# The last layer's attention over batches: one straight program, scores once per head, token-major softmax

## What is computed

```python
def _mha(x, Wqkv, bqkv, Wo, bo):        # L3_ffn: S = 4 batches, B = 512 tokens, H = 4, hd = 32
    qkv = x @ Wqkv.T + bqkv
    ...
    scores = jnp.einsum('bhqd,bhkd->bhqk', q, k) * (1.0 / np.sqrt(hd))
    att = jax.nn.softmax(scores, axis=-1)
    o = jnp.einsum('bhqk,bhkd->bhqd', att, v)
    return o @ Wo.T + bo
...
y = _layer_norm(x + _mha(x, Wqkv, bqkv, Wo, bo), g1, be1)
z = _layer_norm(y + _moe(y, Wg, W1, b1, W2, b2), g2, be2)
```

## Time and profile before

| | |
|---|---|
| median of 3 runs | 2115.09 us (2105.11 to 2148.61) |
| the profiled execution | 2104.8 us, span 2102.9 us |
| PE busy | 1673.5 us (80%), mean granted clock 0.858 |
| DVE busy | 1021.4 us (49%) |
| ACT busy | 722.8 us (34%) |
| POOL busy | 113.1 us (5%) |
| chain that ended last | PE 68%, DVE 20%, ACT 6%, issue 3% |

### The profile page before, as it was taken

The page is one execution under the profiler, slowest core; times in us unless marked ns, Lnnn a source line. Parts: engine busy times, 40 slices in busy tenths (PEclk is TensorE's granted clock), DMA queues, the critical chain, the costliest instruction groups (busy, mean ns, idle before and its releaser), DMA issues.

```text
span 2102.9 us, 22710 instructions
## 1 busy us (share of the span) xinstructions
PE 1673.5 (80%) x9040; PEld 701.1 (33%) x9046; DVE 1021.4 (49%) x2051; ACT 722.8 (34%) x1271; POOL 113.1 (5%) x167
## 2 busy tenths in 40 slices
PE   5559999888998879876489998888987798643385
PEld 2124333333433434322243233334334333211273
DVE  4564662424664641445656624336646414579312
ACT  2332553343343044333325533333430343311132
POOL 0000111000011000000001110000110000000302
PEclk9767999999898779978779998998997799856588
DMA  4000000000001000000000000000000000200141
GB/s 168 1 0 0 1 1 1 1 1 0 1 1 41 0 0 0 1 2 0 0 0 1 1 1 0 1 0 1 2 22 20 0 0 1 69 0 0 60 120 54
DMA packets 17387, 30.29 MB, mean 14 GB/s; under 512 B 1600, under 2 KB 12544, under 8 KB 16384
## 3 DMA queue, kind: packets, MB, share of 16 engines
q1 hardware_dynamic: 16256, 26.72, 3.8%
q0 software_dynamic: 1024, 2.10, 0.3%
HBM read 23.70 MB, written 5.11 MB: 14 GB/s over the span
## 4 chain that ended last, share of the span: by engine, by line
PE 68%; DVE 20%; ACT 6%; issue 3%; POOL 1%; DMA 1%; SPq 0%; POOLq 0%; DVEq 0%; ACTq 0%
PE ps L650 11%; PE ps L703 5%; PE ps L672 4%; PE ps L722 4%; PE ps L509 4%; PE ps L566 3%; PE ps L818 3%; PE ps L831 3%; PE ps L788 3%; PE ps L780 2%; PE ps L587 2%; PE ps L674 2%; PE ps L575 2%; PE ps L541 2%; ACT rs L1190 2%
## 5 line engine op out<-in xcount | busy, mean ns | idle before, releaser
L1255 ACT ACTIVATE big<-ps 128x512 f32<-128x512 f32 (+3 forms) x512 | 238.9, 515 | 257.3 <-PE ps L674 211.2
L650 PE MATMUL ps<-pp,qT 32*128 32x512 f32 (+3 forms) x1024 | 303.0, 632 | 19.5 <-DVE pt L1801 9.0
L672 PE MATMUL ps<-qT,pp 32*128 32x512 f32 (+3 forms) x1024 | 285.2, 580 | 0.0
L1532 DVE TENSOR_REDUCE peak<-ps 128x1 f32<-128x512 f32 x256 | 165.4, 686 | 119.0 <-PE ps L650 118.5
L1529 DVE CUSTOM_DVE_ANT_0 ps<-ps,cst 128x128 f32<-128x128 f32 (+3 forms) x256 | 134.0, 557 | 90.0 <-PE ps L650 87.5
L650 PEld LDWEIGHTS ps<-pp,qT 32*128 32x128 f32 x1024 | 118.8, 206 | 156.8 <-DVE peak L1532 66.0
L1187 ACT ACTIVATE sq<-ps 128x512 f32<-128x512 f32 x60 | 35.8, 597 | 304.3 <-PE ps L509 304.3
L1206 ACT ACTIVATE big<-ps 77x1024 f32<-77x1024 f32 x96 | 94.3, 1019 | 98.5 <-PE ps L566 98.2
L1478 DVE TENSOR_REDUCE small<-ps 128x8 f32<-128x616 f32 x96 | 74.3, 797 | 103.1 <-PE ps L537 57.9
L703 PE MATMUL ps<-big,cst 128*32 128x512 f32 (+3 forms) x1024 | 118.1, 534 | 0.0
L674 PE MATMUL ps<-spare,minus 32*128 32x512 bf16 (+3 forms) x512 | 112.5, 343 | 0.0
(11 more groups left out here) (372 smaller groups left out, 2523.5 us busy)
## 6 DMA issues: line engine op xcount, KB each, us to landing
big<-in_w SPq DMA_DIRECT2D x23, 256.0 KB
pt<-in_l2w SPq DMA_DIRECT2D x2, 2048.0 KB, 7.6
w_l<-in_l SPq DMA_DIRECT2D x1, 3086.0 KB, 18.2
pp<-in_w SPq DMA_DIRECT2D x1, 2048.0 KB, 10.0
cst<-in_const SPq DMA_DIRECT2D x1, 1549.0 KB, 7.0
by_expert<-cst SPq DMA_DIRECT2D x1, 1472.0 KB, 14.0
big<-by_expert SPq DMA_DIRECT2D x23, 64.0 KB, 1.9
w_l<-in_l SPq DMA_DIRECT2D x1, 1218.0 KB, 9.1
```

What stands on the lines that cost most here:

```text
L650: pe.matmul(rbank(x)[:, 0:hi], qT[at, u, 0 if causal else k, 128 * i:128 * i + 128], keyT(u, k)[at, 0:hi], start=True, stop=True, tile_pos ...
L672: pe.matmul(tbank(y)[:, lo:512], keyT(u, k)[at, 128 * j:128 * j + 128], qT[at, u, 0 if causal else k, lo:512], start=True, stop=False, til ...
L1255: A(prob(m)[:, TURN_OF[g], lo:512], tbank(tplace(m, g, causal))[:, lo:512], ACT.Exp)\
L1532: v.tensor_reduce(top, rbank(ring(p, c)), AX.X, ALU.max).then_inc(*VECTOR.did(tag, "max", p, c))
```

## The change

The second loop is gone. The same attention is written as one straight program over the four batches as queries, with no turn ends, and no clearing of semaphores (SP's and POOL's part of them go too).

- A column of 512 is now 512 tokens of one batch, so nothing is copied out of `xall`, and the results are written back and stored as whole batches.
- The norm in front and q, k, v are 4, 4 and 12 matmuls of 128 x 512, as before in number. The v values leave PSUM by ACT, q and k by DVE.
- Products q x k of query batch i with key batches 0 and 1 are on DVE, with 2 and 3 on POOL, whose product is a new kind of instruction there. Each is 128 x 512.
- `score(i)`: four matmuls with 32 columns of weights each, into the four column quarters of one bank: rows are (key batch j, head h, 8 copies). ACT copies it out, PE turns it by four 128 x 128 transposes (`turn_scores`), so that tokens are on partitions, and DVE and ACT do the softmax on 128 x 64 elements (`less_maxima`, `exponentials`, `normalised`) with 16 maxima and sums for each partition.
- The shares go back: four transposes (`turn_shares`), a copy by ACT, and four matmuls with 32 rows of weights each (`spread_shares`, row quarters), which lay each share on the 32 features of its head, one bank for each key batch. DVE multiplies each bank with v (`weigh`, four of 128 x 512).
- The sum over key batches is made in the projection: four matmuls accumulate in one bank (`project`), where one did before.
- The last norm is per batch and interleaved one iteration later (`centred2`, `meaned2`, `norm2`, `normed2`).
- POOL waits for `filled` before its scatter; before, SP waited for it ahead of the turns (and still does).

Added code whole, but for helpers that only name slices; the removed code stands above.

```diff
+def keyed(b):
+    return qT[:, 1, b, :]
+def valued(b):
+    return big[:, b, :]
+def prods(i, j):
+    return big[:, 4 + j, :] if i % 2 == 0 else vt[:, j, :]
+def weighted(j):
+    return flat[:, 2048 + 512 * j:2560 + 512 * j]
...
+spread, expd, most, total = kt_flat[:, 0:128], kt_flat[:, 128:192], kt_flat[:, 192:208], kt_flat[:, 208:224]
+scores, shares, shares_t = xs[:, 0, :], xs[:, 1, :], spare[:, 0:512]
...
+def by_slot(a):
+    return a.rearrange("p (c j h r) -> p c j h r", c=4, j=4, h=4)[:, :, :, :, 0]
...
+def qkv_bank(n):
+    return PSB[(4 + n) % 8]
+QKV = [("k", 0), ("q", 0), ("k", 1), ("k", 2), ("k", 3), ("q", 1), ("q", 2), ("q", 3),
+       ("v", 0), ("v", 1), ("v", 2), ("v", 3)]
...
     sp.wait_ge(filled, 16)
-    with sp.Fori(0, TURNS) as t:
-        end_turn(sp, None, t + 2 + TURNS)
...
-        sp.dma_start(out.rearrange("p (b s) -> p b s", b=B)[:, :, 128 * n:128 * n + 128],
-                     xall[:].rearrange("p (b s) -> p b s", b=B)[:, :, 128 * n:128 * n + 128])\
-            .then_inc(stored, 16)
+        sp.dma_start(out[:, 512 * n:512 * n + 512], x_of(n)).then_inc(stored, 16)
...
-    with pool.Fori(0, TURNS) as t:
-        turn(t + 2 + TURNS)
+    pool.memset(shares, 0.0).then_inc(*POOL.did("l3f zeros"))
+    for i in range(B):
+        pool.wait_ge(*VECTOR["l3f qkv", "q", i])
+        pool.wait_ge(*VECTOR["l3f qkv", "k", 3])
+        if i >= 2:
+            pool.wait_ge(*TENSOR["l3f S", i - 2])
+        for j in (2, 3):
+            ins = pool.tensor_tensor(prods(i, j), qT[:, 0, i, :], keyed(j), ALU.mult)
+        ins.then_inc(*POOL.did("l3f prod", i))
+    pool.wait_ge(*TENSOR["l3f S", 3])
     for k in (3, 5, 15):
         ins = pool.memset(table(k), 0.0)
     ins.then_inc(*POOL.did("moe zeros"))
+    pool.wait_ge(filled, 16)
...
-    with pe.Fori(0, TURNS) as t:
...
-        end_turn(pe, TENSOR, t + 2 + TURNS)
+    for b in range(B):
+        pe.matmul(PSB[b], K["centre"], x_of(b), start=True, stop=True).then_inc(*TENSOR.did("l3f c", b))
+    for b in range(B):
+        pe.wait_ge(*SCALAR["l3f sq", b])
+        pe.matmul(PSB[4 + b], K["mean"], squares(b), start=True, stop=True).then_inc(*TENSOR.did("l3f v", b))
+    for n, (kind, b) in enumerate(QKV):
+        if n < 4:
+            pe.wait_ge(*SCALAR["l3f rs", n])
+        elif n < 8:
+            pe.wait_ge(*VECTOR["l3f n", n - 4])
+        else:
+            pe.wait_ge(*VECTOR["l3f qkv", QKV[n - 8][0], QKV[n - 8][1]])
+        pe.wait_ge(*VECTOR["l3f n", b])
+        at = 128 * "qkv".index(kind)
+        pe.matmul(qkv_bank(n), w["Wqkv"][:, at:at + 128], zs(b), start=True, stop=True)\
+            .then_inc(*TENSOR.did("l3f qkv", kind, b))
+    def score(i):
+        pe.wait_ge(*VECTOR["l3f prod", i])
+        pe.wait_ge(*POOL["l3f prod", i])
+        if i:
+            pe.wait_ge(*SCALAR["l3f scores", i - 1])
+        for j in range(4):
+            mm = pe.matmul(PSB[0][32 * j:32 * j + 32, :], K["head32"][:, 0:128:4], prods(i, j), start=True,
+                           stop=True, tile_position=(0, 32 * j))
+        mm.then_inc(*TENSOR.did("l3f S", i))
+    def turn_scores(i):
+        if i:
+            pe.wait_ge(*SCALAR["l3f shares", i - 1])
+        for c in range(4):
+            mm = pe.transpose(PSB[1][:, 128 * c:128 * c + 128], scores[:, 128 * c:128 * c + 128], ident)
+        mm.then_inc(*TENSOR.did("l3f T", i))
+    def turn_shares(i):
+        pe.wait_ge(*VECTOR["l3f shares", i])
+        for c in range(4):
+            mm = pe.transpose(PSB[1][:, 128 * c:128 * c + 128], shares[:, 128 * c:128 * c + 128], ident)
+        mm.then_inc(*TENSOR.did("l3f back", i))
+    def spread_shares(i):
+        pe.wait_ge(*SCALAR["l3f shares", i])
+        for j in range(4):
+            if i:
+                pe.wait_ge(*VECTOR["l3f weighted", i - 1, j])
+            pe.matmul(PSB[4 + j], spread[32 * j:32 * j + 32, :], shares_t[32 * j:32 * j + 32, :], start=True,
+                      stop=True, tile_position=(32 * j, 0)).then_inc(*TENSOR.did("l3f spread", i, j))
+    def project(i):
+        if i:
+            pe.wait_ge(*SCALAR["l3g ln", i - 1])
+        for j in range(4):
+            pe.wait_ge(*VECTOR["l3f weighted", i, j])
+            mm = pe.matmul(PSB[2], w["Wo2"], weighted(j), start=j == 0, stop=j == 3)
+        mm.then_inc(*TENSOR.did("l3f y", i))
+    def centred2(i):
+        pe.wait_ge(*VECTOR["l3f x2", i])
+        if i:
+            pe.wait_ge(*VECTOR["l3g n", i - 1])
+        pe.matmul(PSB[3], K["centre"], zs(i), start=True, stop=True).then_inc(*TENSOR.did("l3g c", i))
+    def meaned2(i):
+        pe.wait_ge(*SCALAR["l3g sq", i])
+        pe.matmul(PSB[2], K["mean"], squares(i), start=True, stop=True).then_inc(*TENSOR.did("l3g v", i))
+    score(0)
+    turn_scores(0)
+    score(1)
+    for i in range(B):
+        turn_shares(i)
+        if i:
+            centred2(i - 1)
+        spread_shares(i)
+        if i < 3:
+            turn_scores(i + 1)
+        if i:
+            meaned2(i - 1)
+        project(i)
+        if i < 2:
+            score(i + 2)
+    centred2(3)
+    meaned2(3)
+    for n in range(B):
+        pe.wait_ge(*VECTOR["l3g aff", n])
...
-    with act.Fori(0, TURNS) as t:
...
+    exp_set()
+    for b in range(B):
+        act.wait_ge(*TENSOR["l3f c", b])
+        A(squares(b), PSB[b], ACT.Square).then_inc(*SCALAR.did("l3f sq", b))
+    for b in range(B):
+        act.wait_ge(*TENSOR["l3f v", b])
+        A(rstds(b), PSB[4 + b], ACT.Ln, bias=eps).then_inc(*SCALAR.did())
+        act.wait_ge(*SCALAR.last())
+        A(rstds(b), rstds(b), ACT.Exp, scale=-0.5).then_inc(*SCALAR.did("l3f rs", b))
+    for b in range(B):
+        act.wait_ge(*TENSOR["l3f qkv", "v", b])
+        A(valued(b), qkv_bank(8 + b), ACT.Identity, bias=W["l3"]["bqkv"][:, 2:3]).then_inc(*SCALAR.did("l3f value", b))
+    def scores_out(i):
+        act.wait_ge(*TENSOR["l3f S", i])
+        if i:
+            act.wait_ge(*TENSOR["l3f T", i - 1])
+        A(scores, PSB[0], ACT.Identity).then_inc(*SCALAR.did("l3f scores", i))
+    def exponentials(i):
+        act.wait_ge(*VECTOR["l3f sub", i])
+        A(expd, expd, ACT.Exp).then_inc(*SCALAR.did("l3f exp", i))
+    def shares_out(i):
+        act.wait_ge(*TENSOR["l3f back", i])
+        if i:
+            act.wait_ge(*TENSOR["l3f spread", i - 1, 3])
+        A(shares_t, PSB[1], ACT.Identity).then_inc(*SCALAR.did("l3f shares", i))
+    def norm2(i):
+        act.wait_ge(*TENSOR["l3g c", i])
+        A(squares(i), PSB[3], ACT.Square).then_inc(*SCALAR.did("l3g sq", i))
+        act.wait_ge(*TENSOR["l3g v", i])
+        A(rstds(i), PSB[2], ACT.Ln, bias=eps).then_inc(*SCALAR.did("l3g ln", i))
+        act.wait_ge(*SCALAR.last())
+        A(rstds(i), rstds(i), ACT.Exp, scale=-0.5).then_inc(*SCALAR.did("l3g rs", i))
+    scores_out(0)
+    exponentials(0)
+    scores_out(1)
+    for i in range(B):
+        shares_out(i)
+        if i:
+            norm2(i - 1)
+        if i < 3:
+            exponentials(i + 1)
+        if i < 2:
+            scores_out(i + 2)
+    norm2(3)
...
-    with v.Fori(0, TURNS) as t:
...
+    v.tensor_copy(spread.rearrange("p (h f) -> p h f", h=4), K["part"].unsqueeze(2).to_broadcast([128, 4, 32]))
+    for b in range(B):
+        v.wait_ge(*SCALAR["l3f rs", b])
+        v.tensor_tensor(zs(b), PSB[b], rstds(b), ALU.mult).then_inc(*VECTOR.did("l3f n", b))
+    def biased(n):
+        kind, b = QKV[n]
+        v.wait_ge(*TENSOR["l3f qkv", kind, b])
+        at = "qkv".index(kind)
+        v.tensor_scalar(qT[:, at, b, :], qkv_bank(n), w["bqkv"][:, at:at + 1], None, ALU.add)\
+            .then_inc(*VECTOR.did("l3f qkv", kind, b))
+    def products(i):
+        if i >= 2:
+            v.wait_ge(*TENSOR["l3f S", i - 2])
+        for j in (0, 1):
+            ins = v.tensor_tensor(prods(i, j), qT[:, 0, i, :], keyed(j), ALU.mult)
+        ins.then_inc(*VECTOR.did("l3f prod", i))
+    def less_maxima(i):
+        v.wait_ge(*TENSOR["l3f T", i])
+        if i:
+            v.wait_ge(*VECTOR["l3f shares", i - 1])
+        t4 = by_slot(PSB[1])
+        chain(v.tensor_reduce(over_j(most), t4.rearrange("p c j h -> p c h j"), AX.X, ALU.max))
+        v.tensor_tensor(small4(expd), t4, over_j(most).unsqueeze(2).to_broadcast([128, 4, 4, 4]), ALU.subtract)\
+            .then_inc(*VECTOR.did("l3f sub", i))
+    def normalised(i):
+        v.wait_ge(*SCALAR["l3f exp", i])
+        chain(v.tensor_reduce(over_j(total), small4(expd).rearrange("p c j h -> p c h j"), AX.X, ALU.add))
+        chain(v.reciprocal(total, total))
+        if i:
+            v.wait_ge(*TENSOR["l3f back", i - 1])
+        else:
+            v.wait_ge(*POOL["l3f zeros"])
+        v.tensor_tensor(by_slot(shares), small4(expd), over_j(total).unsqueeze(2).to_broadcast([128, 4, 4, 4]),
+                        ALU.mult).then_inc(*VECTOR.did("l3f shares", i))
+    def weigh(i):
+        if i:
+            v.wait_ge(*TENSOR["l3f y", i - 1])
+        for j in range(4):
+            v.wait_ge(*TENSOR["l3f spread", i, j])
```

(67 more changed lines are left out.)

## The result

| | before | after |
|---|---|---|
| median | 2122.74 us (4 runs, 2105.11 to 2148.61) | 2041.63 us (4 runs, 2025.16 to 2047.66) |
| profiled execution, span | 2102.9 us | 2023.2 us |
| first centring (before: first table load) to first logits matmul | 149.2 us | 70.1 us |
| PE, DVE, ACT, POOL busy in it | 65.7, 113.9, 27.5, 0.2 us | 58.7, 41.8, 24.5, 12.5 us |
| mean granted clock in it | 0.68 | 0.91 |

The ratio is **0.963, 95% interval 0.959 to 0.968**: faster, as forecast. Of the 18, 4 are in the stage that was predicted (70.1 for 66).

A forecast was written before the change was run, and what follows sets the result against it. DVE bounded the old 149.2 us loop, PE the new stage: 23.7 + 39.4 = 63.1, plus 3, is 66 us, minus 83. 2104.8 - 83 = 2021.8, with drift 2024 us; own range 2012 to 2040, given range 2010 to 2055.

The forecast's parts named there:

- What bounds it, and what goes: Old attention loop, 1811 to 1960 us: DVE sets the end, PE waits; all 149.2 us are replaced.
- The transfers: Beside the stage: `w2` and `by_expert` loads end by about 1825 us, so POOL's wait for `filled` costs nothing.
- Quarters of the array: Quartered matmuls in `score` and `spread_shares` overlap: 1.1 and 1.15 us per set of four; 3.4 if one after another.
- To the first shares: Stage start until the first softmax is done, before iteration 0: centring, norm, q, k, v, first scores; 23.7 us.
- Neither is late: Before `score(0)`: DVE's and POOL's first products both end at 18.8 us, before PE is free at 19.8.
- Iteration 0: First query batch, from returning the shares through projection and `score(2)` until the next shares can be turned: 7.4 us.
- rival A: PE's clock stays low throughout the stage: 108 + 3 us, a gain of 38, 2067 us in all; 8 in 100.
- Iterations 1 to 3: Remaining query batches with interleaved last norm: 8.9, 8.0 (no score) and 15.1 us (centring waits for the residual).
- The signs: Expected in the stage's profile: POOL's products 1.0 to 1.4 us, projections ending 8 to 9 us apart.
- B: Stage: quarters run one after another (21 us) or 60 hand-overs cost 0.35 us more each; 2043 us; 13 in 100.
- C: POOL's products hold up PE at `score`; whole gain of 83 us gone from 13.3 us a product; 2 in 100.
- D: Behind the stage: experts wait for something formerly hidden, giving the gain back; 2050 us or so; 2 in 100.

## Why the prediction was right, and where it was off

- *What bounds it, and what goes:* right. The 149.2 us were replaced, the stage's new bound is PE, and nothing behind it moved: from the first logits matmul to the end of the span are 142.1 us before and 142.1 after (so the 0.3 us that I allowed the stores isn't seen either).
- *The transfers* cost nothing, as said: their share is 0.00 from 1826 to 1830 us and at most 0.02 behind that, and POOL's wait for `filled` isn't seen.
- *Quarters of the array:* 1.14 and 1.09 us for 1.15 and 1.1 predicted; the spread one by one took 4.8. The experiment confirms what the earlier trace rows let one guess.
- *To the first shares,* 23.7 predicted, 26.9 measured. The step that failed is "Neither is late": I priced POOL's product at 1.03 us and DVE's at 0.68, each alone. POOL's is 1.27 alone and 1.72 beside DVE, DVE's 1.68 beside POOL. That held the first maximum back by 1.8 us (1833.95 to 1835.77), and with 0.75 us for the small product in front of the shares (0.27 without POOL) it makes 2.3 of the 3.2 us; the rest is 0.6 us on PE's way to the transposed scores, from the first centring on, and small steps that took 0.02 to 0.07 us more than priced. The 3 us that I added for "POOL and DVE meeting at the memory" and hand-overs covered this and no more. I had weighed the rule of the Trainium skill (GPSIMD Engine Reference, Specifications: the interface is shared when a VectorE instruction has two SBUF inputs) at 2 us; the trace agrees with the rule. It agrees with its limit too: DVE's biases, which read PSUM, take 0.74 us with POOL beside them for part of their time as without (the second of the two at 1826.78 above), and the small steps with one input from SBUF aren't slowed either.
- *Iteration 0,* 7.4 predicted, 10.0 measured: missed for a reason that I had put into rival A only as all or nothing. In PE's pause of 2.3 us in front of the first shares, a consequence of the collision, the clock fell, and it stayed low for 6.8 us. I counted PE's longest pause as 1.4.
- *Iterations 1 to 3,* 8.9, 8.0 and 15.1 predicted, 9.5, 8.4 and 15.4 measured, 1.2 us more before rounding. In iteration 1 it shows where PE changes between whole and quartered matmuls: the quartered spread starts 0.96 us after the centring, the next transposes 1.07 after the spread, the scores 3.63 after the projection's first (4 x 0.86 = 3.44), the next transposes 1.03 after the scores, where 0.86 is the pace within one form. So a change of form costs 0.1 to 0.2 us; I had read at most 0.1 out of the earlier trace rows. The Trainium skill (TensorEngine Tiling, Key Properties) says that a change of mode drains the engine; the trace agrees.
- *DVE busy* 38 predicted, 41.8 measured. The collision costs more than this difference: with all 16 products on DVE it is 40.5, and 8 of them at 0.62 us are 5, so half of them on DVE undisturbed would have been some 35.5 (an estimate). The collision added about 6, and my other prices were 2 too high (the 16 weighings took 9.9 us for 11.0, the biases 5.4 for 6.0). PE busy 58.7, over the 48 to 56 given: the low clock in iteration 0 is 2.3 of it, since with all products on DVE, at the full clock there, it is 56.3.
- *The signs:* POOL's products took 1.27 to 1.72 us, for 1.0 to 1.4 given, and the projections end 9.5, 9.5 and 8.6 us apart, for 8 to 9.
- *The rivals:* A and B didn't happen as stated, though A's mechanism did for 6.8 us. (A's "0.50 in every long DVE run with PE idle" was too strong: in the kernel before, the windows of 4 us with no matmul at all stand at 0.50 to 0.72.) C: `score(1)` did wait for products, 0.63 us, for DVE's. D: no.
- *The drift:* I added 2 us to the profiled execution; the median lies 16.5 above the profiled one after (2041.6 against 2025.2), 14 more. The profiled execution before was at the fast end of its runs, and so was the one after. So the median is 1.6 us above my own range of 2012 to 2040; that it is inside the range given, up to 2055, is owed to the room left for B, which didn't happen, and is luck in that part.
